# Centring the back's layer norms in the weights, splitting the routing of the gates, and dissolving the first block

## The reference

```python
x = x + L0_xattn(ctx, ctx, ln(x))        # L0X: one head
x = x + L0_ffn(ln(x))                    # L0F: 8 heads; top 2 of 8 experts for the values and for the outputs of each head
x = x + L1_xattn(ln(x), ctx, ctx)        # L1X: 16 heads of 8
x = x + L1_ffn(ln(x))                    # L1F: gelu(x @ fc) -> layer norm -> proj, ternary weights
x = x + L2_xattn(ln(x), ctx, mask)       # L2X: 2 heads of 64, q and k normed per head (eps 1e-6)
x = x + L2_ffn(ln(x))                    # L2F: 8 experts, top 2 by softmax of the logits
x = x + L3_xattn(ln(x), ctx, ctx, bias)  # L3X: 16 heads of 64, scores * D**-0.5 + bias
x = x + L3_ffn(ln(x))                    # L3F: sigmoid gate, group of experts, top 2; relu squared throughout
```

## Time and profile before

| | |
|---|---|
| runs | 757.13 us median of 3 (754.15 to 757.6) |
| the profiled execution | 758.44 us, its span 757.1 us |
| mean granted TensorE clock | 0.943 |
| busy: PE, PEld, DVE, ACT, POOL | 678.2 (90%), 597.5, 522.5 (69%), 380.9, 188.7 us |
| DMA | 113.73 MB, mean 150 GB/s |
| chain that ended last | PE 64%, DVE 15%, ACT 10%, DMA 5% of the span |

### The profile page before, as it was taken

The page is one execution under the profiler, slowest core; times in us unless marked ns, Lnnn a source line. Parts: engine busy times, 40 slices in busy tenths (PEclk is TensorE's granted clock), DMA queues, the critical chain, the costliest instruction groups (busy, mean ns, idle before and its releaser), DMA issues.

```text
span 757.1 us, 14656 instructions
## 1 busy us (share of the span) xinstructions
PE 678.2 (90%) x5474; PEld 597.5 (79%) x5474; DVE 522.5 (69%) x1433; ACT 380.9 (50%) x1291; POOL 188.7 (25%) x260
## 2 busy tenths in 40 slices
PE   4759998989999988899999997899999998977876
PEld 3649996659999987789899986668999996557765
DVE  1935555858668778877578789677767778465756
ACT  2330202782343577745652767654265843755583
POOL 1000004432100400626320413264200514630130
PEclk9969998699999999999999999699999999796997
DMA  9739994029858400767467101085743700000000
GB/s 339 298 116 355 393 351 140 0 58 353 322 210 276 145 1 5 238 209 250 159 203 249 30 2 32 14 256 187 238 160 115 251 29 8 1 1 1 2 1 8
DMA packets 34199, 113.73 MB, mean 150 GB/s; under 512 B 4560, under 2 KB 8272, under 8 KB 33744
## 3 DMA queue, kind: packets, MB, share of 16 engines
q1 hardware_dynamic: 34128, 112.79, 42.9%
HBM read 111.72 MB, written 1.05 MB: 149 GB/s over the span
## 4 chain that ended last, share of the span: by engine, by line
PE 64%; DVE 15%; ACT 10%; DMA 5%; issue 2%; POOL 2%; SPq 0%; DVEq 0%; POOLq 0%
PE f_bank L460 31%; PE bank L460 27%; DMA gated<-gates_of 5%; ACT wide_b L1046 4%; PE bank L655 3%; ACT f_b L983 2%; DVE gated L1335 1%; ACT wide_a L932 1%; DVE f_route L1335 1%; DVE wide_b L1338 1%; POOL rstd L1239 1%; PE bank L644 1%; DVE small L1774 1%; DVE max_neg L1579 1%; ACT f_a L932 1%
## 5 line engine op out<-in xcount | busy, mean ns | idle before, releaser
L460 PE MATMUL f_bank<-weights,gated 128*128 128x128 f32 x2048 | 246.0, 278 | 8.4 <-DVE gated L1335 8.3
L460 PEld LDWEIGHTS f_bank<-weights,gated 128*128 128x128 f32 x2048 | 237.7, 194 | 13.8 <-issue 12.0
L1046 ACT ACTIVATE wide_b<-wide_b,max_neg 128x120 f32<-128x120 f32 x272 | 103.8, 390 | 16.2 <-DVE max_neg L1579 11.8
L1247 POOL TENSOR_TENSOR wide_b<-wide_b,row_inv 128x480 f32<-128x480 f32 x64 | 71.7, 1122 | 124.1 <-DVE row_inv L1584 123.9
L1239 POOL TENSOR_TENSOR rstd<-var_eps,w_const 128x1 f32<-128x1 f32 (+1 forms) x56 | 40.4, 722 | 249.4 <-DVE var_eps L1331 249.1
L1335 DVE TENSOR_TENSOR gated<-gated,f_xnT 128x1024 f32<-128x1024 f32 x64 | 77.6, 1222 | 31.2 <-DMA gated<-gates_of 30.9
L1335 DVE TENSOR_TENSOR gated<-gated,f_b 128x1024 f32<-128x1024 f32 x64 | 77.6, 1232 | 18.0 <-DMA gated<-gates_of 13.3
L932 ACT ACTIVATE wide_a<-bank 120x512 f32<-120x512 f32 (+4 forms) x109 | 58.1, 547 | 61.6 <-PE bank L655 16.7
L1046 ACT ACTIVATION_READ_ACCUMULATOR wide_b<-wide_b,max_neg 128x1 f32 x272 | 53.1, 195 | 0.0
L1204 POOL TENSOR_TENSOR f_rstd<-f_var_eps,w_const 128x1 f32<-128x1 f32 x24 | 13.3, 558 | 149.3 <-DVE f_var_eps L1331 148.8
L655 PE MATMUL bank<-w_const,wide_b 128*120 128x128 f32 x256 | 41.9, 295 | 5.5 <-POOL wide_b L1247 5.4
(11 more groups left out here) (242 smaller groups left out, 1249.7 us busy)
## 6 DMA issues: line engine op xcount, KB each, us to landing
gated<-gates_of SPq DMA_DIRECT2D x128, 512.0 KB, 5.9
weights<-in_experts SPq DMA_DIRECT2D x64, 512.0 KB, 6.4
w_L2f<-in_L2f SPq DMA_DIRECT2D x1, 2124.0 KB, 15.2
w_L3x<-in_L3x SPq DMA_DIRECT2D x1, 2108.0 KB, 19.2
wide_b<-in_raw0f SPq DMA_DIRECT2D x1, 1024.0 KB, 7.9
w_L3f<-in_L3f SPq DMA_DIRECT2D x1, 1000.0 KB, 20.7
w_L1f<-in_L1f SPq DMA_DIRECT2D x1, 516.0 KB, 10.5
x_next<-in_x SPq DMA_DIRECT2D x4, 128.0 KB, 5.6
```

The lines of the kernel that those rows point to most:

```text
L460: return nc.tensor.matmul(o, lhsT, rhs, start=first, stop=last)
L1046: last = nc.scalar.activation(p, p, ACT.Exp, bias=max_neg[lane][:, h:h + 1], accum_out=row_sum[lane][:, h:h + 1])
L1247: nc.gpsimd.tensor_tensor(p3, p3, row_inv[lane][:, 4 * i:4 * i + 4].unsqueeze(2).broadcast_to([128, 4, K]), ALU.mult).then_inc(probs_norme ...
```

## The change

It has these parts.

1. **Centred weights.** In L1F, L2X, L3X and L3F the weights that act on the norm are multiplied once, in `late_setup`, with a centring matrix (`centre` is the identity minus 1/128, `centre_heads` the same per head of 64), which takes the mean off. `turn_x` then turns `x` itself as soon as it is written, and 1/sqrt(var+eps) is applied behind the product: as the scale of L1F's Gelu, in the scores of L2X (per head, with a suitably scaled eps) and of L3X, in the gate's exponential and, squared, at the output of L3F. L1X and L2F keep the normed rows. Seven copies of centred weights, six products of TensorE up to 512 columns wide, and two small ones are added to the setup; they wait for the loads of L2x, L3x and L3f.
2. **L2X.** The queries come out of TensorE twice, transposed for the scores and plain for the statistics; the norming, turning and copying of `small` are gone. The probabilities are turned as they are, and 1/sum is applied to the output, one head at a time. Keys and folded values of L2X come before L1F, and the values and keys of L3X behind them, in bank 2.
3. **Gates.** The routing of L0F is split into two halves: top two and gates of the values (`best_two(0)`, `gates(0)`) stand ahead of the first maxima; those of the outputs stand between and behind. `turn_gates(0)` stands between the two halves of the scores, and the second half waits for `f_gateT_ready[0]`. SP's queue is unchanged here.
4. **L2F.** The gate's exponential is a power on GpSimd (base e) and not an ACTIVATE. The expert sums are split 4, 2, 2, and the bias product goes to bank 0.
5. **L3F.** The sum of the two best per group is the largest of six pair sums. **Softmaxes**: the third bank's scores are taken before the first reciprocals.
6. **Folding.** The first block is dissolved into the streams; the two warming products of 512 columns (`keep_warm`) are gone; `raw0x`, `x` and the context are loaded first. Masks of pair p+1 are made during the L2F of pair p.
7. The tables `ORDER` are new for all engines. A line of each:

```diff
-    "PE": "fffff0f0ffff0fffffffffff0fffffffffffffffffffffffffffffffffffffffffff011fffffff1f0f0fff1ff1f10ff0f10f"
+    "PE": "fff0ffffff0f0f0ffff0ffff0f00fff0ffffffffffff0fffffffffffffffffffffffffffff0f010f1fff0f0ff10f00f1fff0"
...
                     def turn_x(lane, layer, rows):

                         if layer == L1X:
                             pe.wait_ge(f_mid_ready[lane], f_mid_ready.upto(L1X, 1, pair))
+                        elif layer == L2F:
+                            pe.wait_ge(xn_ready[lane], xn_ready.upto(L2F, 1, pair))
                         else:
-                            pe.wait_ge(xn_ready[lane], xn_ready.upto(layer, 1, pair))
+                            pe.wait_ge(x_ready[lane], x_ready.upto(layer - 1, 1, pair))
...
+                    centre = part["const", "centre"]
+                    pe.wait_ge(qk_taken, 2)
+                    mm(bank[0][2][:, :], centre, part["L1f", "fc"]).then_inc(centre_products, 1)
+                    pe.wait_ge(loaded["L2x"], 16)
+                    mm(bank[1][2][:, 0:D], part["L2x", "wq"], centre).then_inc(centre_products, 1)
+                    yield
+                    pe.wait_ge(loaded["L3x"], 16)
+                    pe.wait_ge(setup_taken, PROJ_MEAN)
+                    for half in range(2):
+                        mm(bank[half][1][:, :], centre, part["L3x", "wq"][:, 512 * half:512 * half + 512])\
+                            .then_inc(centre_products, 1)
+                    yield
...
+                    def turn_gates(t):
+                        pe.wait_ge(f_gates_ready[t], pair + 1)
+                        nc.tensor.transpose(f_bank[0][:, 0:S], f_gate[:, 128 * t:128 * t + 128], ident)\
+                            .then_inc(f_gateT_psum[t], 1)
                     for half in range(2):
+                        if half == 1:
+                            pe.wait_ge(f_probs_ready[0], f_probs_ready.upto(L0F, 1, pair))
+                            turn_gates(0)
+                            yield
                         for lane in LANES:
                             if half == 0:
                                 pe.wait_ge(f_q_ready[lane], f_q_ready.upto(L0F, 2, pair))
                             else:
                                 pe.wait_ge(f_probs_ready[lane], f_probs_ready.upto(L0F, 1, pair))
+                                if lane == 0:
+                                    pe.wait_ge(f_gateT_ready[0], pair + 1)
...
-                    mm(bank[lane][1][:, 0:D], xnT[lane][:, :], part["L2x", "wq"]).then_inc(q_psum[lane], 1)
-                    yield
-                    pe.wait_ge(normed[lane], normed.upto(L2X, 2, pair))
-                    nc.tensor.transpose(bank[lane][0][:, 0:S], small[lane][:, 0:D], ident).then_inc(turned_psum[lane], 1)
-                    yield
-                    pe.wait_ge(turned_ready[lane], turned_ready.upto(L2X, 2, pair))
+                    mm(bank[lane][0][:, 0:S], part["L2x", "wq"], xnT[lane][:, :]).then_inc(q_psum[lane], 1)
+                    mm(bank[lane][1][:, D:2 * D], xnT[lane][:, :], part["L2x", "wq"]).then_inc(q_psum[lane], 1)
+                    yield
...
-                    nc.scalar.activation(wide_b[lane][:, 0:512], bank[lane][1][:, :], ACT.Gelu)\
+                    nc.scalar.activation(wide_b[lane][:, 0:512], bank[lane][1][:, :], ACT.Gelu, scale=rstd[lane][:, 0:1])\
                         .then_inc(hidden_ready[lane], 1)
...
+                    pool.wait_ge(max_taken[lane], max_taken.upto(L2F, 1, pair))
+                    below_max = route[:, 1, E * lane:E * lane + E]
+                    nc.gpsimd.tensor_tensor(below_max, part["const", "euler"], below_max, ALU.pow)\
+                        .then_inc(gate_pow[lane], 1)
...
+                    yield from best_two(0)
+                    ins = yield from gates(0)
+                    ins.then_inc(f_gates_ready[0], 1)
+                    yield
                     for lane in LANES:
                         maxima(0, lane)
                         yield
-                    dve.wait_ge(f_top_exp, pair + 1)
...
+                    yield from best_two(1)
                     for lane in LANES:
                         maxima(1, lane)
                         yield
-                    dve.wait_ge(f_gates_ready[0], pair + 1)
+                    ins = yield from gates(1)
+                    link(ins)
+                    yield
...
                     for h in range(H2X):
-                        last = tt(wide_b[lane][:, K * h:K * h + K], bank[lane][h][:, 0:K], mask2[lane][:, :], ALU.add)
+                        last = stt(wide_b[lane][:, K * h:K * h + K], bank[lane][2 * h][:, 0:K], rstd[lane][:, h:h + 1],
+                                   mask2[lane][:, :], ALU.mult, ALU.add)
...
-                    for h in range(H2X):
-                        p = wide_b[lane][:, K * h:K * h + K]
-                        last = ts(p, p, row_ok[lane][:, 2 + h:3 + h], row_inv[lane][:, h:h + 1], ALU.mult, ALU.mult)
-                    last.then_inc(normed[lane], 1)
-                    yield
-                    add_output(lane, L2X, bank[lane][1][:, 0:D])
-                    yield
...
+                    link(stt(x[lane][:, :], bank[lane][0][:, 0:D], row_inv[lane][:, 0:1], x[lane][:, :], ALU.mult, ALU.add))
+                    x_done(lane, L2X, stt(x[lane][:, :], bank[lane][0][:, D:2 * D], row_inv[lane][:, 1:2], x[lane][:, :],
+                                          ALU.mult, ALU.add))
```

708 lines of the change are left out of this document (385 added, 323 removed).

## The result

The changed kernel took 735.01 us (median of 4 runs, 734.56 to 737.88) beside 755.64 us (751.88 to 757.6) of the kernel before; the ratio of the runs is 0.9741 with a 95% interval of 0.9691 to 0.979. A second comparison gave 0.9762 (0.9727 to 0.9797). The forecast was 740 us, with a range of 727 to 754. The span of the profiled execution is 734.1 us.

A forecast was written before the change was run, and what follows sets the result against it. Bounds: DMA in the first expert phase, TensorE's work in later ones, the front's chain in the gaps. Start 55.0 + first phase 67.1 + gaps 157.5 + later phases 347 + tail 112.6 = 739.2, given as 740 us, range 727 to 754.

The forecast's parts named there:

- lane 1's lead: Tail: lane 1, a layer ahead, fills waits of lane 0's L2X with eight products of 128 columns, 1.8 us.
- The start, 55.0: Up to the first expert product: 54.3 us before, +0.7 from later exponentials; bounds -4 to +3.
- VectorE carries what follows and has more ahead of it: Start: dissolving the folding block could free up to 8 us, but none is credited; VectorE first works on L1F's weights at 18.42.
- Value gates first: Start: both stores precede the first spread on SP's queue, so having the value gates first gives the DMA nothing.
- (a): Four softmaxes: the wait for the turned value gates shows in every pair, 3.3 us each, 753 us in all; chance 0.12.
- (b): Same wait, stronger: the copy queues behind back work, second scores slip, gaps cost 59, total 762 us; chance 0.06.
- Gaps and later phases, 504.5: Three gaps at 52.5 each, 157.5, and later expert phases 347; 5.6 us less than 510.1 before.
- I allow 1%: Later expert phases: time over TensorE's work, 0.4% before, taken as 1%, so 343.4 x 1.01 = 347 us.
- The tail, 112.6: Last back without a front: 125.6 less 13, of which 9.0 from seams and similar, 4 from TensorE's work and lane 1.
- Rival (c), the clock: Fuller queues keep full clock for half of 66 us at half clock; up to 16 us back, 724; chance 0.12.
- Rival (d): Seams were hidden: tail 121.5 by TensorE's work and the lanes' exchange, gaps stay at 54, total 753.4 us; chance 0.10.
- Rival (e): First front: without the two wide warming products the clock falls, 7 us, half hidden, total 744; chance 0.04.

The follow-up runs named there:

- fold_first: Changed kernel with SyncE's loads in the old order and queries and keys folded ahead of the front's first product; 740.91 us, ratio 0.9799 to the kernel before.
- gates_late: Changed kernel with the value gates turned and copied with the output gates, behind the exponentials; 751.87 us, ratio 0.9975 to the kernel before.
- gates_middle: Changed kernel with the value gates turned behind both halves of the scores, ahead of the turning of probabilities; 743.57 us, ratio 0.9863 to the kernel before.
- seam_stats: Changed kernel, but in L1F, L2X, L3X and L3F TensorE turns rows centred by VectorE behind the statistics; 748.04 us, ratio 0.9898 to the kernel before.
- side_by_side: Changed kernel, but in the last back lane 1's L2F stands behind lane 0's L2X on four engines; 744.78 us, ratio 0.9879 to the kernel before.
- warm_tail: Changed kernel plus three 512-column products on constants in each of two TensorE waits of the last back; 734.56 us, ratio 0.9719 to the kernel before.
- after_again: The changed kernel unaltered, executed again beside the other runs; span 734.0 us, ratio 0.9762 to the kernel before.
- warm_later: Changed kernel plus warming products in the last back and queries and keys folded behind the front's whole L0X; 731.88 us, ratio 0.9709 to the kernel before.

## Why the prediction was right, step by step

The total came out 5 us under the forecast, inside the range, and the tail and the gaps went the way that was forecast: the seams and lane 1's lead shorten the tail, and back work moved out of the gaps. But the terms are off in both directions (start 4.2, first phase 3.0, gaps 3.8 and tail 1.8 us too long, later phases 7.7 too short), so that it came this near is in part luck.

**The start, 55.0: 50.8, wrong by 4 (by 2 to 4 over its executions).** The step that failed is "I give it none, because VectorE carries what follows and has more ahead of it". `fold_first` puts the dissolved block at about 3 us of the start; with the folding ahead of the front, the case that 55.0 was worked out for, the start took 56.1. I had read VectorE's 18.42 as the arrival of L1F's weights. It was a place in the queue: in the timeline of before it stands directly behind the front's first norm, in the changed kernel at 17.46 behind the front's `x`, and 5.1 us later in `fold_first`. In the changed kernel the load takes 10.3 us from its issue at 6.10, so it is there at 16.4. The routing's price was too low: the operations that I put at 0.28 us took 0.29 in the first front but 0.353 in the mean, so 1.5 us more a pair and not 0.6. Together with the other operations over `f_route` VectorE has 35.2 us instead of 25.1, 2.5 more a pair, where I had 2 with all small ones.

**Value gates first.** The prediction had it that they give the DMA nothing, which holds (the store's landing is on the chain only in `gates_late`), and concluded that the place brings nothing, which does not. `gates_middle` costs 8 us: what the early turning frees, as its timeline of the first front shows, is TensorE's and ScalarE's path from the last exponentials to the turned probabilities. That the gaps lose by the same path is argued from this front. The rivals (a) and (b) looked at the wait that the order adds (1.33 us in the start, 0.6 and 0.5 in two gaps, 0 in one) and not at the one that it takes away.

**The first expert phase, 67.1:** 64.1, by chance of the execution that was profiled; before had 67.1 and 64.3, and the later runs with the changed kernel's instructions there 64.5 to 66.5.

**Gaps and later phases, 504.5: 508.4.** The gaps came at 51.2 on average, 1.3 under the 52.5 each; the phases at 354.7 for 347. Nearly the whole excess is in the second: 123.5 us for 115.5 of work. TensorE is idle for 4.2 us of it, and the hole from 252.7 to 276.2, in which no expert product runs, has some 7 us at half clock (2 x 0.15 x 23.5), 3.5 of work, behind a wait of 2.79 us for GpSimd. There GpSimd's scalings of 128x480 and VectorE's expert tiles slow each other:

```profile
246.09 0.99 POOL L1317 TENSOR_TENSOR wide_b<-wide_b,row_inv 128x480 f32<-128x480 f32 x1 [10.39 <-DVE row_inv L1680]
248.90 10.53 POOL L1317 TENSOR_TENSOR wide_b<-wide_b,row_inv 128x480 f32<-128x480 f32 x6 [0.45 <-DVE row_inv L1680]
250.00 5.71 DVE L1413 TENSOR_TENSOR gated<-gated,f_b 128x1024 f32<-128x1024 f32 x3
```

One scaling takes 0.99 us alone and 1.76 in the mean of this row of six (the five beside expert tiles 1.9, the last again 0.98), an expert tile 1.90 us instead of 1.22. By the Trainium skill's page "SBUF — State Buffer", section "SBUF: two separate sides", the two engines share a port pair that one instruction holds as "an exclusive lock", which blocks a VectorE instruction with two inputs from SBUF against a GpSimd one that reads there. The rows agree that both are held up, but not with a lock over whole instructions: one of each would then take 0.99 + 1.22 = 2.21 us, and both engines finish one in 1.9.

The step of the prediction that failed is "I allow 1%" over the work of the later phases. Such meetings were there before too (scalings of 1.87 to 1.89 us from 600 to 607 us), but in none of these phases is TensorE shown waiting for them. The prediction also had it that on GpSimd "no gap's chain hangs on them more than before"; for TensorE's turning of probabilities the wait for GpSimd's scaling grew from 5.4 us (3.8 in the second execution) to 14.2 (14.6), first row before, second row changed:

```profile
L655 PE MATMUL bank<-w_const,wide_b 128*120 128x128 f32 x256 | 41.9, 295 | 5.5 <-POOL wide_b L1247 5.4
L679 PE MATMUL bank<-w_const,wide_b 128*120 128x128 f32 x256 | 44.4, 307 | 14.3 <-POOL wide_b L1317 14.2
```

Of the 14.2 us 6.1 are in the tail and 8.1 ahead of it. This is a candidate for what ate the gain of the shorter seams in gaps and later phases: seams about 0.9 us longer cost 9.8 us there, and yet seams about 2 us shorter than before brought next to nothing. No run took it apart, so that stays open. One reading of the sum was wrong as well: L2X has 2 more products and 2 fewer transposes in each pair (16 and 8 instructions over all four), not 8, which is 0.2 us a pair; the rest of the +2.8 is a counting difference at the marks or other work.

**The tail, 112.6: 110.8.** Right in sum and wrong in its parts. Seams were to give 8.6 times 0.85; the share that `seam_stats` measured is 0.5 to 0.6 (0.2 at the least), so 4 to 5. Lane 1's lead was to give 2, beside 2 for the smaller work; `side_by_side` measures 6.8. With 1.9 us of work that is 13 to 14 of 14.8 to 16.6; the rest (the queries' path, the pair sums of L3F, the clock) was not taken apart. The step that failed is the one on lane 1: it priced the eight products that fill a wait, and not that the lanes side by side stand in line for TensorE afterwards, at half clock first.

**Rival (c), the clock,** came true in part: the tail's half-clock time fell from 35 to 2 x 0.08 x 110.8 = 18 us, and the mean clock rose from 0.943 to 0.965. TensorE is busy for 11.9 us less (666.4 for 678.2) with 3 us more to do. In `warm_tail` 11 us less at half clock gave 2.4 us. Rival (d) is refuted by `seam_stats`. Rival (e) isn't borne out. Between 20 and 40 us the clock is shown as 0.83 where it was 0.99,

```profile
20.00:40.00 20.00, 18.33 (x105) 14.96 (x105) 17.94 (x51) 9.88 (x41) 0.00 (x0) 0.83 0.66 275
20.00:40.00 20.00, 14.54 (x95) 12.27 (x96) 17.61 (x45) 7.46 (x28) 1.13 (x2) 0.91 0.57 243
```

but the kernel before, with its two wide products, has 0.91 in its second execution (second row), and the 0.99 that the prediction leaned on is no measurement, as the last section shows: there the wide products themselves ran at half pace. Whether dropping them costs anything was tested by no run. Whether the clock is a cause of what the tail won or follows from shorter waits isn't settled either; the run meant for it in the kernel before didn't fill the wait.

**What single parts are worth** can't be added up: undoing the start's part costs 3 to 4 us, the gates' place 8, the lanes' lead 9, and under half of the 2.2 us of each seam 10, in sum some 30 us where the whole change is worth 20. The order table was fitted to all of them together, and each kernel with one part undone runs with a table made for another.

## What to carry over

Waits at the head of an in-order queue cost even where the engine looks busy all the time: the longer seams cost 6.3 us in three expert phases in which TensorE was busy for 96% of the time or more. When a step is moved, price the wait that disappears behind it as carefully as the one that appears ahead of it. And before a late engine is called the bound, look for the row in which it waits for its data; a place in a queue looks the same in a list of start times.

## What was unexpected in the hardware

**The same code comes out with another clock in another execution.** The second expert phase's hole took 23.5 us at a clock of 0.85 and the gap behind it 50.8 at 0.97 in `after_again`; in `side_by_side`, whose instructions are the same there, 20.8 at 1.00 and 53.4 at 0.90:

```profile
257.30:278.10 20.80, 17.82 (x171) 15.44 (x170) 10.19 (x37) 12.32 (x33) 7.88 (x7) 1.00 0.12 49
290.50:343.90 53.40, 47.34 (x312) 34.03 (x312) 43.20 (x139) 39.57 (x157) 20.88 (x30) 0.90 0.13 34
```

The sums are 74.3 and 74.2 us, so here the neighbour took back what the hole had won. It doesn't always: `warm_later`, again with the same instructions, has 22.4 and 50.7, in sum 73.1. A stretch of one execution is thus known to 2 or 3 us where the clock changes in it, although the total repeats.

**The clock of the start is shown as 1.00 where it was half.** Each pair of rows is the same work, in the changed kernel and in `seam_stats`, and in the first and the second execution of before:

```profile
15.07 1.06 PE L441 MATMUL bank<-wide_b 128*128 128x128 f32 x8
15.77 1.91 PE L441 MATMUL bank<-wide_b 128*128 128x128 f32 x8
23.75 2.90 PE L460 MATMUL bank<-w_const 128*128 128x512 f32 x4
21.32 1.88 PE L460 MATMUL bank<-w_const 128*128 128x512 f32 x4
```

All four stretches are shown with a granted share of 1.00. By the pace of the products TensorE came to full rate at about 13 us in the changed kernel and at about 30 in `seam_stats`, which no share tells. Such a late rise goes with a start of 53.3 us instead of 50.7 to 51.9, and what decides on it is open. The shares of the start, and the means over the span, are therefore too high; the durations of equal instructions are the safer witness.
